# Output projection of the third layer: four row tiles, four PSUM banks

## What is computed

```python
q = (x @ Wq.T).reshape(B, N, NUM_HEADS, HEAD)
k = (x @ Wk.T).reshape(B, N, NUM_HEADS, HEAD)
v = (x @ Wv.T + bv).reshape(B, N, NUM_HEADS, HEAD)
a = jnp.einsum('bnhd,bmhd->bhnm', q, k) * SCALE + encoding_bias[:, None, :, :]
...
a = jax.nn.softmax(a, axis=-1)
o = jnp.einsum('bhnm,bmhd->bnhd', a, v).reshape(B, N, HIDDEN)
return o @ Wo.T + bo
```

## Time and profile before

| | us |
|---|---|
| median of 3 runs | 2781.34 (2780.72 to 2782.75) |
| the profiled execution, its own time | 2777.82 |
| its span | 2776.0 |
| PE busy in the span | 2648.7 |
| VectorE busy in the span | 1959.0 |

### The profile page before, as it was taken

One profiled execution on the slowest core, in us unless ns is written; L12 is line 12 of the kernel. 1 busy time (PEld: TensorE's weight loads), 2 busy tenths in 40 slices (PEclk: granted clock), 3 DMA queues, 4 the chain that ended last, 5 costly groups with the idle time before them and its releaser, 6 DMA issues. The chain is left out here.

```text
span 2776.0 us, 60158 instructions
## 1 busy us (share of the span) xinstructions
PE 2648.7 (95%) x23616; PEld 2294.6 (83%) x23616; DVE 1959.0 (71%) x4530; ACT 1247.0 (45%) x2433; POOL 1405.2 (51%) x1287
## 2 busy tenths in 40 slices
PE   8999999999959999999999959999999999999997
PEld 7999898999847788888888848888888888888886
DVE  6788888888864565555656548777777876777776
ACT  2344344444433344444444434445444454555554
POOL 6756655765646666666666635323222323343333
PEclk9999999999989999999999979999999999999999
DMA  5011121221123111111111020111111111112111
GB/s 156 30 52 56 57 73 31 68 64 43 57 70 105 35 55 35 47 47 35 58 36 54 24 75 32 51 51 51 31 46 51 51 51 51 51 51 75 51 51 60
DMA packets 152425, 150.29 MB, mean 54 GB/s; under 512 B 74704, under 2 KB 150096, under 8 KB 152144
## 3 DMA queue, kind: packets, MB, share of 16 engines
q1 hardware_dynamic: 152144, 146.45, 17.4%
HBM read 96.09 MB, written 50.33 MB: 53 GB/s over the span
## 5 line engine op out<-in xcount | busy, mean ns | idle before, releaser
L1655 POOL TENSOR_TENSOR h_logits<-h_logits,h_mx 128x512 f32<-128x512 f32 x192 | 201.9, 1052 | 539.1 <-DVE h_mx L1514 539.1
L917 DVE TENSOR_TENSOR l_val<-l_ring,l_vec 64x384 f32<-64x384 f32 x512 | 284.5, 556 | 74.9 <-PE l_ring L730 67.9
L730 PE MATMUL l_ring<-whi,l_hhi 128*128 128x384 f32 x1152 | 275.4, 347 | 5.7 <-POOL wlo L68 5.7
L730 PE MATMUL l_ring<-wlo,l_hhi 128*128 128x384 f32 x1152 | 263.1, 336 | 0.0
L730 PE MATMUL l_ring<-whi,l_hlo 128*128 128x384 f32 x1152 | 262.8, 336 | 0.0
L1250 PE MATMUL h_ring<-h_hhi,whi 128*128 128x512 f32 x576 | 240.5, 417 | 11.8 <-DVE h_zb L1564 5.8
L1250 PE MATMUL h_ring<-h_hlo,whi 128*128 128x512 f32 x576 | 227.9, 396 | 0.0
L1250 PE MATMUL h_ring<-h_hhi,wlo 128*128 128x512 f32 x576 | 227.6, 395 | 0.0
L730 PEld LDWEIGHTS l_ring<-whi,l_hhi 128*128 128x128 f32 x1152 | 198.7, 189 | 30.7 <-issue 18.6
L398 DVE TENSOR_TENSOR l_val<-l_ctx,l_vec 128x384 f32<-128x384 f32 x128 | 70.5, 556 | 211.1 <-PE l_ctx L262 210.7
L339 ACT ACTIVATE l_sides<-l_ring 128x512 f32<-128x512 f32 x192 | 114.2, 595 | 207.0 <-PE l_ring L278 207.0
(11 more groups left out here) (239 smaller groups left out, 6636.9 us busy)
## 6 DMA issues: line engine op xcount, KB each, us to landing
l_hf<-xt SPq DMA_DIRECT2D x16, 864.0 KB, 4.9
l_x<-x SPq DMA_DIRECT2D x16, 768.0 KB, 4.6
l_x<-x SPq DMA_DIRECT2D x32, 384.0 KB, 3.1
h_xa<-x SPq DMA_DIRECT2D x32, 384.0 KB, 5.1
h_xb<-x SPq DMA_DIRECT2D x32, 384.0 KB, 5.1
x<-l_zfa SPq DMA_DIRECT2D x8, 768.0 KB, 3.5
x<-l_zfb SPq DMA_DIRECT2D x8, 768.0 KB, 4.3
x<-l_za SPq DMA_DIRECT2D x8, 768.0 KB, 3.5
```

The source lines that it names most:

```text
L730: mm = nc.tensor.matmul(ring[k % RING][:, 0:D], hh[:, c, first:first + P], ww[:, c, :], start=(j == 0), stop=(j == len(terms) - 1))
L917: ins = nc.vector.tensor_tensor(val[half, (g + b) % GRAPHS, 0:D], ring[k % RING][half, 0:D], bias[half, :], ALU.add)
L1655: nc.gpsimd.tensor_tensor(row, row, mx[:, c, :, ts].unsqueeze(3).broadcast_to([P, HP, 2, S]), ALU.subtract).then_inc(sub_done, 1)
```

## The change

The four row tiles of the projection go into ring[0], ot[1], ot[0] and ring[1] instead of ring[0], ring[1], ot[1] and ring[0]. Five waits on PE follow from that: those of `query_key` for its first two products, the two of `output` for tiles 0 and 1, and those of `result`.

```diff
--- before.py
+++ after.py
@@ -1138,7 +1138,7 @@
 
         row_banks = (pt[0], pt[1], ot[0])
         output_banks = (pt[0], pt[1], ot[0], ot[1])
-        result_banks = (ring[0], ring[1], ot[1], ring[0])
+        result_banks = (ring[0], ot[1], ot[0], ring[1])
 
         vec_in = sem("vec_in")
         col_in = sem("col_in")
@@ -1240,7 +1240,7 @@
                 if k >= 2:
                     pe.wait_ge(qk_evac, 2 * KC * n + k - 1)
                 elif project(n - 2):
-                    pe.wait_ge(w_evac, T * (n - 2) + (4, 2)[k])
+                    pe.wait_ge(w_evac, T * (n - 2) + (1, 4)[k])
                 else:
                     pe.wait_ge(v_evac, max(T * (n - 1) + 3 + k, 0))
                 for c in range(KC):
@@ -1303,8 +1303,8 @@
                 pe.wait_ge(n_done, max(T * n + t - 1, 0))
                 if t == 0 and n + 1 < slots:
                     pe.wait_ge(lo_done, KC * (n + 2))
-                if t == 1 and project(n - 1):
-                    pe.wait_ge(w_evac, T * (n - 1) + 3)
+                if t < 2 and project(n - 1):
+                    pe.wait_ge(w_evac, T * (n - 1) + 3 - t)
                 for m in range(PAIRS):
                     for b in range(2):
                         rows = slice(S * b, S * b + S)
@@ -1324,12 +1324,12 @@
 
             def result(n, t):
                 pe.wait_ge(olo_done, T * n + t + 1)
-                if t < 2:
-                    pe.wait_ge(v_evac, T * (n + 1) + 3 + t)
-                elif t == 2:
+                if t in (0, 3):
+                    pe.wait_ge(v_evac, T * (n + 1) + 3 + t // 3)
+                elif t == 1:
                     pe.wait_ge(olo_done, T * (n + 1))
                 else:
-                    pe.wait_ge(w_evac, T * n + 1)
+                    pe.wait_ge(lo_done, KC * (n + 3))
                 row_major(lambda c: ohi[:, t, c, :], lambda c: olo[:, t, c, :], weight(n, 3), result_banks[t][:, 0:D])\
                     .then_inc(w_done, 1)
```

## The result

The changed kernel takes 2765.74 us (median of 4 runs, 2764.52 to 2766.87), the kernel before 2781.91 in the same measurement (2780.72 to 2782.75). The ratio is 0.9941 with a 95% interval of 0.9929 to 0.9953. The medians differ by 16.2 us; by the interval the gain is between 13 and 20. The forecast was 2765.5.

The account below looks back on a forecast made before the run. PE, in its own order, was taken to bound the projection's slots, with one stall before line 1250. 15.8 for the removed wait less 0.0 for the added one took the median from 2781.34 to 2765.5 us, range 2761.5 to 2771.5.

Parts of the forecast that it names:

- What bounds the kernel: Third layer's projection, slots 1 to 16: PE runs back to back except 0.72 us idle before line 1250, 11.6 us.
- rival (c): Another engine paces the slot, its wait grows elsewhere on PE and the time does not move: 2781, chance 0.02.
- The wait removed: query_key(n + 1, 0) waits only for result 0's addition: 0.88 plus 0.11, together 0.99 us a slot, 15.8 us.
- the refilling of the array after standing still: First query matmul after the stall holds the second back 0.34 instead of 0.23: 0.11 us a slot.
- rival (a): Only the idle time before the query projection comes back and the new wait costs its bound: 10.2 us, 2771.1, chance 0.07.
- The next waits: Later waits on the same banks are satisfied: query_key(n + 1, 1) with 1.25 to spare, result 2 with 1.74.
- rival (b): Stall moves to query_key(n + 1, 1); a slip of 1.75 us leaves half the gain, 7.9 us: 2773.4, chance 0.03.
- The wait added: output(n, 0) gets a fifth condition, for result 2's addition, satisfied long before; cost 0.00.
- the bound of 0.09: Upper bound on the added condition at output(n, 0): the handover's whole loss against the 0.23 pitch, 1.4 us in all.
- What is late next: After the query projection no other wait takes over; ACT's idle at query 0's evacuation falls from 2.07 to 1.08.
- The sum: 15.8 - 0.0 = 15.8 us over 16 slots; the median goes from 2781.34 to 2765.5, 0.57% less.

Follow-up runs that it names:

- Experiments 1: Changed kernel, but query_key(n + 1, 0) again waits for all four additions into z; 2781.84 us, against 2782.03 for the kernel before.
- 2: Changed kernel, but query_key(n + 1, 0) waits for three additions into z; 2774.02 us, ratio to the kernel before 0.9972.
- 4: Changed kernel with bank order ot[0], ot[1], ring[0], ring[1], so result 0 waits for the next rows' low parts; 2792.87 us.
- Experiment 5: Changed kernel plus eight more already satisfied waits in front of output(n, 0), 16 times; 2766.06 us.
- experiment 3: Changed kernel with results 0 to 2 back in their old banks and only result 3 moved, into ot[0]; 2765.58 us, ratio 0.994.

## Why the prediction was right

- *What bounds the kernel.* PE, in the order in which its work is written. Experiments 1, 2 and 4 add 0.99 (16 times), 0.52 (15 times) and 1.64 us (16 times) to PE's slots, 15.8, 7.8 and 26.2 us, and the medians move by 16.1, 8.3 and 27.1, within 1 us of each. Nothing was taken up elsewhere, which also rules out rival (c).
- *The wait removed.* 0.88 and 0.11 were forecast; the starts show 1.40 - 0.52 = 0.88 and 0.34 - 0.23 = 0.11. The size of the 0.11 was right; its name, the refilling of the array after standing still, was not quite (see the last section). The choice between the idle time (11.6 us) and the starts (15.8 us) was the one that mattered, and experiment 2 decides it against rival (a) in a second place.
- *The next waits.* query_key(n + 1, 1) has no entry in the list of waits, so rival (b) did not happen. Its first matmul, the tenth of the query products, starts at 1762.94, 1.27 after result 3's addition has ended at 1761.67; 1.25 was forecast. How much later the addition could come was not tried. Result 2 starts at 1757.72 and its low parts are there at 1755.97: 1.75 to spare, 1.74 was forecast. Experiment 4 shows what would have happened without that slack.
- *The wait added.* Forecast at nothing, against the bound of 0.09. The fifth condition added no instruction (60158 before and after), so there was nothing to pay. Experiment 5 adds 64 wait instructions in the same place and finds nothing that can be measured. Its trace says why: the six wait instructions ahead of output(n, 0), each 0.05 long, start between 1769.41 and 1769.94, while PE still works on the matmuls ahead, and the output starts at 1772.31. In all 16 slots they are passed at least 2.1 us before it. The Trainium skill (Perfetto Trace Analysis, Identifying Dependency Chains) says that an instruction which waits on several engines may get extra semaphore instructions in front of it. The trace agrees for the eight conditions of experiment 5, and they had no price that these runs could measure.
- *What is late next.* On ACT the evacuation of query 0 idles 1.08 for PE, as forecast:

```profile
1763.14 0.60 ACT L1402 ACTIVATE h_q<-h_ring 128x512 f32<-128x512 f32 x1 [1.08 <-PE h_ring L1250]
```

- *The sum.* 15.8 us, and 15.8 between the first and the last query matmul; 16.2 between the medians. That the forecast median, 2765.5, came within 0.3 of the measured one is in part luck: it started from 2781.34, where the kernel before has 2781.91 in the measurement beside the changed one, and the runs of the changed kernel spread over 2.4.

## What to carry to other kernels

When an in-order engine waits at the same place in every slot, ask which buffer it wants and who used it last; here one tile of four stood in the bank that the next product needed, and giving that tile a bank that is needed later (ring[1] in the change, ot[0] in experiment 3) brought all of the gain. Price such a stall from start to start of the engine's instructions, not from the idle column, and then look for the next wait on every buffer that has taken the tile. A freed buffer is only free if its own reader is done when the tile comes: the order of the tiles over the same four banks decided between 0.6% faster and 0.3% slower.

## What I had not expected

A stall of PE costs more than it shows: 0.24 us of idle time in the profile cost 0.52 (experiment 2), 0.72 cost 0.99 (the kernel before). The surplus is nearly the same, 0.27 to 0.28: 0.16 for the last matmul that runs out uncovered and 0.11 for the slower first step after it.

The rows of the weight loads (PEld, which puts the weights of a matmul into the array while earlier matmuls run) show what is slow in that step. Of the kernel before, then of the changed kernel:

```profile
1760.46 0.19 PEld L1250 LDWEIGHTS h_ring<-h_hhi,whi 128*128 128x128 f32 x1 [1.04 <-DVE h_zb L1564]
1760.57 0.19 PEld L1250 LDWEIGHTS h_ring<-h_hlo,whi 128*128 128x128 f32 x1
```

```profile
1760.67 0.19 PEld L1250 LDWEIGHTS h_ring<-h_hhi,whi 128*128 128x128 f32 x1
1760.84 0.19 PEld L1250 LDWEIGHTS h_ring<-h_hlo,whi 128*128 128x128 f32 x1
```

In the changed kernel the first query matmul's load starts 0.17 ahead of it (1760.67, 1760.84). Behind the stall load and matmul start together at 1760.46, since the load had to wait too; the second load follows 0.11 later, and the second matmul 0.23 after its load in both kernels. Standing still is not needed for this: behind the turned probabilities in the kernel before, with no idle time, the load is only 0.03 ahead (1769.26, 1769.29) and the first step takes 0.32. Behind the scores the load is not ahead either (1754.49, with the matmul, in the changed kernel), and the first group of results is slow in any case (1754.49 to 1755.12, 0.63 instead of 0.52); there a stall brought no second surcharge: 0.60 in experiment 4. That the late load is the cause is read from these starts; no run varied it alone.

The distance from the end of VectorE's record to PE's next start was 0.04 behind an addition into z and 0.15 behind a low part. Why they differ was not tried.
